# Cross-attention and a gated FFN on one core: the FFN's head products in plain float32 instead of three float16 products

## The reference

```
def ffn(x, Wq, Wk, Wv, Ws, Wd, Wo):            # H = 16 heads, DH = 64, E = 8 experts, K = 2
    q = einsum('btc,hdc->bhtd', x, Wq)
    k = einsum('btc,hdc->bhtd', x, Wk)
    gate_v = einsum('btc,hec->bthe', x, Ws)
    w, sel = top_k(gate_v, K)                  # the two best experts of each token and head
    mix_v = einsum('bthk,bthke->bthe', sigmoid(w), one_hot(sel, E))
    proj_v = einsum('btc,edc->bted', x, Wv)
    v = einsum('bthe,bted->bhtd', mix_v, proj_v)
    probs = softmax(einsum('bhid,bhjd->bhij', q * DH**-0.5, k))
    attn = einsum('bhij,bhjd->bihd', probs, v)
    mask_o = the two best of einsum('btc,hec->bthe', x, Wd), as ones and zeros
    return einsum('bthe,bthd,efd->btf', mask_o, attn, Wo)

x = x + cross_attention(layernorm(x), ctx, ...)
x = x + ffn(layernorm(x), ...)
```

## Time and profile before

| | us |
|---|---|
| median of three runs | 469.22 |
| lowest and highest run | 467.35, 471.89 |
| the profiled execution: its own time | 469.56 |
| its span, first to last instruction | 467.7 |
| mean granted TensorE clock | 0.973 of full speed |
| PE busy | 412.8 (88% of the span) |
| PE weight loads busy | 359.2 (77%) |
| DVE busy | 404.1 (86%) |
| ACT busy | 337.7 (72%) |
| POOL busy | 133.6 (29%) |
| median distance of two runs of L919 in the loop | 16.28 |

### The profile page before, as it was taken

How to read it: one execution, slowest core, us unless ns; L and a number is a source line. 1 busy time by engine, 2 the same in 40 slices (tenths; PEclk the granted TensorE clock), 3 DMA queues, 4 the chain that set the end, 5 groups by cost and what they waited for, 6 DMA issues and landing times.

```text
span 467.7 us, 25765 instructions
## 1 busy us (share of the span) xinstructions
PE 412.8 (88%) x10859; PEld 359.2 (77%) x10859; DVE 404.1 (86%) x775; ACT 337.7 (72%) x924; POOL 133.6 (29%) x142
## 2 busy tenths in 40 slices
PE   1877999999999986578999999999999999999985
PEld 1666789889889875557878788787878878787874
DVE  6897788998989943779999999999999999999962
ACT  6585788788788653366776697688769767876872
POOL 7645788889888650000000000000000000000000
PEclk9999999999999987598999999999999999999999
DMA  7972965465460000000000000000000000000000
GB/s 174 362 239 78 281 208 201 139 204 196 136 202 0 1 4 1 1 1 5 3 7 0 5 5 5 0 5 5 0 5 5 5 0 5 5 2 2 8 8 13
DMA packets 18158, 29.51 MB, mean 63 GB/s; under 512 B 3017, under 2 KB 14025, under 8 KB 18121
## 3 DMA queue, kind: packets, MB, share of 16 engines
q1 hardware_dynamic: 18120, 28.97, 19.5%
HBM read 28.05 MB, written 0.92 MB: 62 GB/s over the span
## 4 chain that ended last, share of the span: by engine, by line
DVE 41%; PE 30%; ACT 13%; issue 12%; DMA 2%; SPq 1%; DVEq 1%; ACTq 0%
DVE ctxf_all L960 9%; DVE ctxf_all L934 6%; PE ps L1062 5%; DVE attnf L971 4%; ACT pf L511 4%; DVE ah L988 4%; PE ps L1296 2%; PE ps L1095 2%; PE ps L1109 2%; ACT e_sb L609 2%; PE ps L1110 2%; PE ps L1111 2%; ACT p L514 2%; PE ps L1077 2%; ACT ctxT L505 2%
## 5 line engine op out<-in xcount | busy, mean ns | idle before, releaser
L609 ACT ACTIVATE e_sb<-ps,smn 128x56 f32<-128x56 f32 x256 | 76.4, 374 | 0.4 <-DVE smn L978 0.4
L609 ACT ACTIVATION_READ_ACCUMULATOR e_sb<-ps,smn 128x1 f32 x256 | 67.2, 274 | 0.0
L960 DVE TENSOR_TENSOR ctxf_all<-mixp,diag_h 128x3584 f16<-128x3584 f16 x32 | 63.2, 2017 | 0.0
L391 POOL TENSOR_TENSOR nat<-ctxf_all,nat 128x640 f16<-128x640 f32 x32 | 55.0, 1719 | 22.8 <-ACT nat L500 22.7
L1062 PE MATMUL ps<-ident,nat 128*128 128x128 f16 x768 | 56.7, 223 | 5.3 <-DVE ctxT L736 2.8
L397 POOL TENSOR_TENSOR p<-pf,p 128x672 f16<-128x672 f32 x32 | 55.3, 1728 | 18.9 <-ACT p L514 18.8
L1062 PEld LDWEIGHTS ps<-ident,nat 128*128 128x128 f16 x768 | 45.0, 99 | 8.1 <-issue 6.5
L500 ACT CAST nat<-ctxf_all 128x1536 f16<-128x1536 f32 x32 | 47.5, 1483 | 4.0 <-DMA ctxf_all<-in_ctx_dram 2.9
L736 DVE COPY ctxT<-ps 128x1024 f16<-128x1024 f16 x64 | 42.3, 681 | 1.7 <-PE ps L1062 1.7
L511 ACT ACTIVATE pf<-ps 128x672 f32<-128x672 f32 x32 | 23.7, 740 | 25.6 <-PE ps L1095 25.6
L1231 PE MATMUL ps<-xn,mT 128*128 128x112 f16 x256 | 41.1, 219 | 0.0
(11 more groups left out here) (172 smaller groups left out, 1235.0 us busy)
## 6 DMA issues: line engine op xcount, KB each, us to landing
ctxf_all<-in_ctx_dram SPq DMA_DIRECT2D x32, 704.0 KB
ctxf_all<-in_ctx_dram SPq DMA_DIRECT2D x32, 46.0 KB
x_all<-in_x_dram SPq DMA_DIRECT2D x4, 224.0 KB
out_dram<-y_all SPq DMA_DIRECT2D x32, 28.0 KB
ctxf_all<-in_ctx_dram SPq DMA_DIRECT2D x32, 18.0 KB
fwq_nat<-in_L_ffn_Wq_dram SPq DMA_DIRECT2D x1, 512.0 KB, 6.2
fwk_nat<-in_L_ffn_Wk_dram SPq DMA_DIRECT2D x1, 512.0 KB, 6.1
fwv_nat<-in_L_ffn_Wv_dram SPq DMA_DIRECT2D x1, 256.0 KB, 5.9
```

Of the source, the lines that this page charges most:

```text
L391: pool.tensor_tensor(nat[k][:, 1, 7 * C:], ctxf[k][:, 7 * C:], nat[k][:, 0, 7 * C:], ALU.subtract).then_inc(natlo2, 1)
L609: last = act.activation(e_sb[:, k, b, 0:S], ps[:, b, S * k:S * k + S], ACT.Exp, bias=smn[:, K16 * b + k:K16 * b + k + 1], scale=-1.0, accu ...
L960: last = dve.tensor_tensor(dv[:, part, :, :, :], mixp[:, part, :, :].unsqueeze(2).broadcast_to((P, 2 * NQ, HALF, H)), diag_h[:, :, :].unsq ...
```

## The change

The head matrices are kept as one float32 tensor `mT` of 16 matrices, and the products of `z_heads` read it and the float32 tokens `xnT`, which are there already. One product for each head replaces three. ACT's float16 copy of the tokens (L587), DVE's `low_tokens` (L926), DVE's low halves of the matrices (L864) and their three semaphores go. PE's waits on the two float16 token tensors become a wait on the float32 copy (`f_xnTe`), which is issued ahead of both.

```diff
-        mT = sb("mT", [P, 2, H, C], F16)
+        mT = sb("mT", [P, H, C])
-        xn16 = sb("xn16", [P, 2, 2 * S], F16)
...
-            mT_v = mT[:, 0, :, :].rearrange("p (a k h) c -> p h a k c", a=2, h=2)
+            mT_v = mT[:, :, :].rearrange("p (a k h) c -> p h a k c", a=2, h=2)
...
             def xnT_evac(i):
...
                 act.copy(xnT[:, 0:2 * S].rearrange("p (b t) -> p b t", b=2),
                          ps[:, 5, 0:P].rearrange("p (b t) -> p b t", b=2)[:, :, 0:S]).then_inc(f_xnTe, 1)
-                act.copy(xn16[:, 0, :].rearrange("p (b t) -> p b t", b=2),
-                         ps[:, 5, 0:P].rearrange("p (b t) -> p b t", b=2)[:, :, 0:S]).then_inc(f_xh, 1)
...
-            for h2 in range(2):
-                dve.wait_ge(fp_act, 4 + h2)
-                for a in range(2):
-                    last = dve.tensor_tensor(mT_v[:, 1, h2, a, :, :], ps[:, 4 * h2 + a, :].rearrange("p (k c) -> p k c", c=C),
-                                             mT_v[:, 0, h2, a, :, :], ALU.subtract)
-                last.then_inc(fp_dve, 1)
...
-            def low_tokens(i):
-                after(dve, f_xh, i + 1)
-                after(dve, f_s, i)
-                dve.tensor_tensor(xn16[:, 1, :]..., ALU.subtract).then_inc(f_xl, 1)
...
-                if nxt:
-                    low_tokens(i + 1)
...
-                    pe.matmul(o, mT[:, 0, h, :], xn16[:, 0, :], start=True, stop=False)
-                    pe.matmul(o, mT[:, 0, h, :], xn16[:, 1, :], start=False, stop=False)
-                    last = pe.matmul(o, mT[:, 1, h, :], xn16[:, 0, :], start=False, stop=True)
+                    last = pe.matmul(o, mT[:, h, :], xnT[:, 0:2 * S], start=True, stop=True)
...
-                    after(pe, f_xh, i + 1 if front else i)
-                    after(pe, f_xl, i + 1 if front else i)
+                    after(pe, f_xnTe, i + 1 if front else i)
...
-                    after(pe, f_xh, i + 1)
-                    after(pe, f_xl, i + 1)
+                    after(pe, f_xnTe, i + 1)
...
-            pe.wait_ge(fp_dve, 2)
```

More of the change, by code:

```diff
@@ L190, in xattn_ffn @@
         fp_act = sem("fp_act")
-        fp_dve = sem("fp_dve")
-        f_xh = sem("f_xh")
-        f_xl = sem("f_xl")
         ln_sqrt = sem("ln_sqrt")
@@ L857, in _ @@
                 step(u, u % DEEP)
-            mT_v = mT[:, :, :, :].rearrange("p s (a k h) c -> p s h a k c", a=2, h=2)
-            for h2 in range(2):
-                dve.wait_ge(fp_act, 4 + h2)
-                for a in range(2):
-                    last = dve.tensor_tensor(mT_v[:, 1, h2, a, :, :], ps[:, 4 * h2 + a, :].rearrange("p (k c) -> p k c", c=C),
-                                             mT_v[:, 0, h2, a, :, :], ALU.subtract)
-                last.then_inc(fp_dve, 1)
             dve.wait_ge(mvd, NP)
@@ L920, in mixing @@
                                   ALU.mult).then_inc(f_mix, 1)
-            def low_tokens(i):
-                after(dve, f_xh, i + 1)
-                after(dve, f_s, i)
-                dve.tensor_tensor(xn16[:, 1, :].rearrange("p (b t) -> p b t", b=2),
-                                  ps[:, 5, 0:P].rearrange("p (b t) -> p b t", b=2)[:, :, 0:S],
-                                  xn16[:, 0, :].rearrange("p (b t) -> p b t", b=2), ALU.subtract).then_inc(f_xl, 1)
             def masks(i):
@@ L999, in _ @@
             normalise(0)
-            low_tokens(0)
             top_two(0)
```

## The result

The changed kernel took 490.81 us (median of four runs, 488.97 to 492.22) against 468.69 us for the kernel before on the same chip. The ratio is 1.046, with a 95% interval of 1.040 to 1.052. A second series of five gave 489.86 us, ratio 1.044 (1.040 to 1.048). The forecast was 486.4 us in a range of 480 to 490. The direction is right, and the time lies 0.8 us above the range and 4.4 us above the forecast. The profiled execution took 488.97 us; its span is 487.2 us, 19.5 more than before, where 17.2 were forecast.

A forecast was written before the change was run, and what follows sets the result against it. DVE's chain was taken to set the 16.3 us loop period, with PE's path 0.06 us behind; +17.9 + 1.4 - 2.0 - 0.14 = +17.2 us gave 486.4 us, 3.7% slower, range 480 to 490.

The forecast's parts named there:

- Two records a product, 112 ns each, set by the load: In z_heads, 16 float32 products make 32 load-bound records, 3.57 us to the last start against 2.32, +1.25 us a pair.
- The rival of the moving columns: In z_heads, moving columns set a record's time, 96 ns; z_heads +0.75 us a pair, 478.2 us in all; chance 9%.
- PE's path has about 0.06 us of slack: Between mix and L978 in the loop, z_heads growth beyond 0.06 us moves L978 and the period.
- L978 moves by +1.19 us: The minima on DVE start 1.19 us later a pair; 15 pairs make +17.9 us.
- low_tokens gives -0.14: Removing low_tokens between L978 and mix lets L988 start 0.14 us earlier in 14 iterations, -2.0 us.
- Iteration 0, +1.4: z_heads at half clock in iteration 0, all on the path, adds 1.4 us, range +1.25 to +2.8.
- The passage, -0.14: Without the matrices' low halves (L864), the square root waits only for ACT's table load, 0.14 us earlier.
- the sum itself: Over the whole kernel, the terms +17.9, +1.4, -2.0 and -0.14 add up to +17.2 us.

The follow-up runs named there:

- e4_half: The changed kernel with only the first 56 of the 112 token columns multiplied in z_heads, same loads; 493.28 us.
- e6_strips: The changed kernel with each head's stationary matrix loaded in two strips of 64 columns, twice the products; 481.49 us, ratio 1.028.
- e7_four: The kernel before with a fourth float16 product a head (low times low), 64 records in place of 48; 485.2 us, ratio 1.034.
- e3_keeplow: The changed kernel with ACT's float16 token copy, DVE's low_tokens and PE's waits on them put back; 493.08 us.
- e1_again: The changed kernel run and profiled once more, no edit; 489.86 us.
- e2_fill32: The changed kernel with 32 tiny float32 products on PE at the very start; 486.41 us, ratio 1.036.
- e8_best: The kernel before with mix fused into one DVE operation, low tokens made on GpSimd and ACT's float16 copy later; 467.58 us, ratio 0.997.
- e11_fused: The kernel before with only mix fused into one DVE operation, low_tokens left on DVE; 465.84 us, ratio 0.995.
- e12_pool_late: The kernel before with only low tokens moved to GpSimd and ACT's float16 copy later, mix as it was; 469.94 us, ratio 1.004.
- e10_two: The kernel before with two float16 products a head, high times low left out, 32 records in place of 48; 470.16 us, ratio 1.004.
- e9_fill64: The changed kernel with 64 tiny float32 products ahead of the loop, 32 at the start and 32 later; 492.48 us, ratio 1.050.
- e5_before_fill32: The kernel before with 32 tiny float32 products on PE at its start; 474.85 us, ratio 1.011.

## Why the prediction was right, and where it failed

- *Two records a product, 112 ns each, set by the load:* right. Last start after 3.56 us (3.57 forecast). e4_half kept the pace with half the columns, and e6_strips broke the bound as the rows said, to 96 ns. The rival of the moving columns is out.
- *PE's path has about 0.06 us of slack:* right for the minima (e7_four added 0.79 us and moved them by 0.74), wrong for the period. The low halves (L988) start 1.32 us behind the scores' end in the kernel before, and 1.33 in e7_four, where they wait for ACT's cast. The cast follows ACT's copy of the next tokens (L585), which waits for PE's work right behind the scores (L1224), and on that way there was no slack to take off.
- *L978 moves by +1.19 us:* measured +1.24 (mix to minima 6.66 before, 7.90 after). From the first z record to L1320's first it is 3.75 against 2.46, +1.29, as the next group starts 0.19 behind the last float32 record and 0.14 behind the last float16 one. The forecast had taken the distance of last starts.
- *low_tokens gives -0.14:* right. Keeping it costs 0.15 (e3_keeplow), and the step's mechanism, ACT's cast ending last, is in the chain after. L964 starts 1.17 us behind the scores' end, for which the forecast had 1.14, and 1.32 without the removal, where it had 1.28. The period was forecast at 16.28 + 1.25 - 0.06 - 0.14 = 17.33 and is 16.28 + 1.29 - 0.15 = 17.42: 0.09 us a pair too little, 0.06 of it the slack.
- *Iteration 0, +1.4:* between mix and minima 8.39 before; 9.07, 10.27 and 9.87 in after, e1_again and e2_fill32, +0.7 to +1.9, as the half clock ends at different moments.
- *The passage, -0.14:* right. The root stands right behind the table load, 1.29 us behind its start in place of 1.42. The profiled execution reaches it 1.29 us earlier in all, and the rest came ahead of it: head_products started 0.93 us earlier, where the kernel before ran near half clock (0.61 and 0.53 from 172 to 176 us, 1.00 after), and its second group took 2.05 us in place of 2.28.
- **The step that failed** is the sum itself: it took the kernel to be unchanged outside z_heads, the token copies and the passage, and so put the straight code behind the loop at nothing. The runs showed stalls in PE's instruction supply there: 4.4 us in the profiled execution and 3.3 us in e1_again by the lengths of the two groups, 3.5 us by the medians of e1_again and e2_fill32. I counted what each product costs, but not that 4 x 32 records fewer move every later instruction by half a 16 KB piece. With the stalls gone (e2_fill32) the kernel takes 486.41 us.

That 486.41 meets the forecast of 486.4 is partly luck, since other errors cancel. The table puts the forecast against the two profiled executions, from start to start.

| stretch | forecast, us | measured, us |
|---|---|---|
| start to mix of iteration 0 | -0.14 | -1.29 |
| mix of iteration 0 to that of iteration 1 | +1.4 | +0.67 (17.10 to 17.77) |
| the next two distances | +2.1 | +0.81 (16.82 and 17.06 to 17.24 and 17.45) |
| the 12 distances up to iteration 15 | +12.6 | +13.7 |
| from there to the end | +1.2 | +5.65, 4.4 of it the stalls |
| sum | +17.2 | +19.5 |

In the two distances of the third row the kernel before was slower than its 16.28 us a pair: its granted clock was 0.75 and 0.82 from 208 to 216 us (1.00 in the changed kernel), and it had the stop at record 25 of the scores in iteration 2. The forecast charged 15 pairs as if all were steady. The stop is there at the same record in e8_best, e11_fused and e12_pool_late, which have the same records on PE; the clock is low there in e8_best too, 0.79, and at 1.00 in e11_fused and e12_pool_late.

That the first median was another microsecond above the second is within what the series scatter.

## What to carry to other kernels

Count a float32 product by its load: with a 128-column stationary operand and fewer than 128 moving columns the load sets the pace, so three float16 products can be cheaper than one float32 product, and splitting the float32 one into two column strips gives part of it back. Where two engines' paths between the same two points are within 0.1 us of each other, time added to either arrives whole (0.79 us in e7_four) and time removed from one returns next to nothing (0.05 of 0.71 in e10_two). And when a change alters the number of instructions ahead of a straight stretch with dense groups, look for gaps without a releaser inside a group in both traces, and move the ends of the pieces with a filler before judging the change by a per cent.

## What the runs showed of the hardware

Instructions come over a DMA queue of their own. The DMA view of the changed kernel, first over 200 us of the loop and then from 450 us to the end:

```profile
q1 hardware_dynamic: 1540, 0.63, 1.2%
```

```profile
q1 hardware_dynamic: 560, 0.23, 2.4%
q8 instruction: 5, 0.08, 0.9%
```

In these 200 us of the loop no instruction packet moves, with some 860 records of PE in each pass (e2_fill32 has a single one in its loop, at 277 us); behind it there are 5 packets of 16 KB, and PE executes 1,312 records there, 5.1 times 256. 16 KB is 256 instructions of 64 bytes if a record is one, as e9_fill64 and the 512 instructions between two stops bear out. The Trainium skill ("Runtime: NRT & Kernel Launch", section on instruction fetch mechanics) gives PE room for 2,048 instructions, refilled in blocks of 256. The quiet loop agrees with that, and not with the same section's remark that only two blocks are held. The same section of the Trainium skill also says that the refill is hidden since instructions issue slowly. Here it is not: attention times values runs its 256 records in 1.48 us, and the stop of PE in its middle lasts 2.1 to 2.6 us.

The packets stand close to these stops. In the nine traces with a stop in the last attention times values, a 16 KB packet starts between 0.35 us before the stop and 0.25 us behind its start, takes 0.9 to 1.2 us, and PE goes on 1.3 to 1.6 us after its end. In the changed kernel the packet is at 475.01 to 475.89 us, inside the stop from 474.77 to 477.42:

```profile
q8 instruction: 1, 0.02, 2.1%
```

That it holds what PE waits for is likely but not shown.

All twelve kernels, and the two they come from, fit one rule. Those whose count of loads and passes up to the last scores differs from the kernel before by a multiple of 256 (itself, e2_fill32, e8_best, e11_fused, e12_pool_late) run through behind the loop; those that differ by 128 more or less (the changed kernel, e1_again, e3_keeplow, e4_half, e5_before_fill32, e6_strips, e7_four, e9_fill64, e10_two) stop for 2 us or more. But the end of a piece inside a dense group is not enough for a stop. Half a piece away from records 22 and 105, the kernels that run through have their ends at about record 86 of one attention times values and record 40 of the next, and run over both without a gap. What more it takes, and when a packet is asked for, is open; no run tried it.
